# Experts' token transposes moved behind the up products, two experts ahead

## What is computed

```python
xn = layernorm(x)
attn = einsum('bsr,or->bso', rfs(xn, xis, exp(xis), proj), rfs(iw, xis, exp(xis), proj))
# mixture of experts
scores = sigmoid(tokens @ router_w)            # 4 of 8 groups, then 8 of 64 experts
dispatch = dispatch.at[flat_e, pos_c].add(tokens[tidx] * valid[:, None])   # 256 rows an expert
g = einsum('ech,ehi->eci', dispatch, gate_w)   # 512 -> 256
u = einsum('ech,ehi->eci', dispatch, up_w)     # 512 -> 256
expert_out = einsum('eci,eih->ech', silu(g) * u, down_w)                   # 256 -> 512
output = zeros.at[tidx].add(gathered * weights)
output = output + (silu(tokens @ sg) * (tokens @ su)) @ sd
return x + attn + output
```

## Time and profile before

| | |
|---|---|
| median of 3 runs | 1327.19 us (1311.12 to 1372.49) |
| profiled execution | 1307.97 us |
| its span | 1306.2 us |
| granted TensorE clock, mean | 0.996 |
| PE busy | 1280.0 us (98%) |
| DVE busy | 916.0 us (70%) |
| ACT busy | 647.3 us (50%) |
| POOL busy | 433.9 us (33%) |
| moved by DMA | 263.65 MB, mean 202 GB/s |
| DMA rate in the experts' half | 277 to 298 GB/s by slice |

### The profile page before, as it was taken

The page is one execution under the profiler, slowest core; times in us unless marked ns, Lnnn a source line. Parts: engine busy times, 40 slices in busy tenths (PEclk is TensorE's granted clock), DMA queues, the critical chain, the costliest instruction groups (busy, mean ns, idle before and its releaser), DMA issues.

```text
span 1306.2 us, 22561 instructions
## 1 busy us (share of the span) xinstructions
PE 1280.0 (98%) x7565; PEld 1123.8 (86%) x7565; DVE 916.0 (70%) x1787; ACT 647.3 (50%) x1053; POOL 433.9 (33%) x344
## 2 busy tenths in 40 slices
PE   6999999999999999999999999999999999999995
PEld 5888888888888888888889999999999999999994
DVE  7878877777777777785656667667766766676662
ACT  4421232212322123221256777777877777777772
POOL 1000000000000000000014666777666667676653
PEclk9999999999999999999999999999999999999998
DMA  7336554664546645445447999999999999999995
GB/s 269 121 107 163 130 121 127 157 166 98 130 119 153 167 104 131 114 118 134 134 133 214 286 278 286 287 290 292 290 291 285 298 291 287 282 295 285 298 277 65
DMA packets 203800, 263.65 MB, mean 202 GB/s; under 512 B 49268, under 2 KB 138744, under 8 KB 203768
## 3 DMA queue, kind: packets, MB, share of 16 engines
q1 hardware_dynamic: 175096, 191.93, 50.9%
q0 software_dynamic: 28672, 71.32, 23.7%
HBM read 178.18 MB, written 71.39 MB: 191 GB/s over the span
## 4 chain that ended last, share of the span: by engine, by line
PE 96%; DVE 2%; DMA 1%; ACT 0%; issue 0%; POOL 0%; SPq 0%; ACTq 0%
PE pmm L1255 18%; PE pmm L1257 18%; PE pmm L1256 18%; PE pout L1255 11%; PE pout L1257 11%; PE pout L1256 11%; PE ptr L1488 4%; PE plog L1316 2%; PE plog L1325 1%; PE ptr L1267 0%; DMA out_dram<-outs,slot_cols 0%; DVE stats L829 0%; DMA xbuf<-_L_attn_proj_matrix_dram 0%; DVE xt_lo L795 0%; PE plog L1345 0%
## 5 line engine op out<-in xcount | busy, mean ns | idle before, releaser
L1614 POOL DMA_INDIRECT out_dram<-outs,slot_cols x128 | 228.7, 1787 | 165.6 <-DMA out_dram<-outs,slot_cols 136.2
L1255 PE MATMUL pmm<-xt_hi,proj_hi 128*128 128x256 f32 (+1 forms) x784 | 253.0, 323 | 2.2 <-DVE xt_lo L795 1.4
L1257 PE MATMUL pmm<-xt_hi,proj_lo 128*128 128x256 f32 (+1 forms) x784 | 249.6, 318 | 0.0
L1256 PE MATMUL pmm<-xt_lo,proj_hi 128*128 128x256 f32 (+1 forms) x784 | 249.6, 318 | 0.0
L1255 PE MATMUL pmm<-xt_hi,sgu_hi 128*128 128x256 f32 (+1 forms) x768 | 246.1, 320 | 0.2 <-issue 0.2
L1256 PE MATMUL pmm<-xt_lo,sgu_hi 128*128 128x256 f32 (+1 forms) x768 | 243.4, 317 | 0.0
L1257 PE MATMUL pmm<-xt_hi,sgu_lo 128*128 128x256 f32 (+1 forms) x768 | 243.4, 317 | 0.0
L1598 POOL TENSOR_TENSOR earlier<-earlier,chosen 128x64 bf16<-128x64 bf16 x64 | 23.9, 373 | 617.8 <-DVE chosen L916 614.0
L1604 POOL DMA_INDIRECT xbuf<-rows,slot_cols x128 | 175.3, 1369 | 80.8 <-issue 38.6
L552 ACT ACTIVATE feat<-pmm,ab 128x512 f32<-128x512 f32 x68 | 46.7, 687 | 292.4 <-PE pmm L1257 286.4
L1255 PEld LDWEIGHTS pmm<-xt_hi,proj_hi 128*128 128x128 f32 x784 | 147.3, 188 | 13.6 <-ACT feat L552 1.6
(11 more groups left out here) (185 smaller groups left out, 2543.7 us busy)
## 6 DMA issues: line engine op xcount, KB each, us to landing
raw<-in_L_ffn_gate_w_dram SPq DMA_DIRECT2D x64, 512.0 KB
raw<-in_L_ffn_up_w_dram SPq DMA_DIRECT2D x64, 512.0 KB
raw<-in_L_ffn_down_w_dram SPq DMA_DIRECT2D x64, 512.0 KB
outs<-in_L_attn_x_dram SPq DMA_DIRECT2D x32, 512.0 KB, 3.9
out_dram<-outs SPq DMA_DIRECT2D x32, 512.0 KB, 3.0
xbuf<-in_L_attn_x_dram SPq DMA_DIRECT2D x52, 256.0 KB, 7.6
raw<-xn SPq DMA_DIRECT2D x52, 256.0 KB, 6.2
rows<-raw SPq DMA_DIRECT2D x39, 256.0 KB, 4.2
```

What stands on the lines that cost most here:

```text
L1255: pe.matmul(psum, lh, rh, start=first and n == 0, stop=False)
L1256: pe.matmul(psum, lh, rl, start=False, stop=False)
L1257: ins = pe.matmul(psum, ll, rh, start=False, stop=final and n == len(pairs) - 1)
L1614: pool.indirect_dma_start(out=out, out_offset=bass.IndirectOffsetOnAxis(ap=slot_cols[:, at:at + 1], axis=0), in_=outs[e.b][:, c, :], in_of ...
```

## The change

The transposes move in the queues of three engines, and are made one expert further ahead. On TensorE they stand between the up products and the down products, for expert e + 2. On ScalarE the copy to `xt_hi` stands behind the rounding of the down weights; on VectorE `xt_lo` stands behind the hidden product, and the down weights' residual moves ahead of the hidden product. The first two sets of transposes are read out ahead of the first stage, and the last stages leave theirs out.

```diff
--- before.py
+++ after.py
@@ -738,12 +738,12 @@
                         e_out_made, 1)
 
             def stage(e, next_rows=True, next_weights=True, out_prev=True, look=None):
-                if next_rows:
-                    e_turned_hi(e.next())
                 if next_weights:
                     gate_up_hi(e.next())
                 e_silu(e)
                 down_hi(e)
+                if next_rows:
+                    e_turned_hi(e.next().next())
                 e_hidden_hi(e)
                 if out_prev:
                     e_out(e.prev())
@@ -751,6 +751,7 @@
                     sum_signs(look)
 
             e_turned_hi(turn(0))
+            e_turned_hi(turn(1))
             stage(turn(0), next_weights=False, out_prev=False)
             for b in range(2):
                 act.wait_ge(out_stored[b], 16 * GROUPS)
@@ -759,7 +760,7 @@
                 for k in range(CHUNK):
                     stage(four(2 * m + 1, k), look=m + 2 if k == 1 else None)
             for n in range(E - 6, E - 1):
-                stage(turn(n))
+                stage(turn(n), next_rows=n < E - 2)
             stage(turn(E - 1), next_rows=False, next_weights=False)
             e_out(turn(E - 1))
 
@@ -1224,18 +1225,19 @@
                                   ALU.subtract).then_inc(e_hid_lo_made, 1)
 
             def stage(e, next_rows=True, next_weights=True, look=None):
-                if next_rows:
-                    e_turned_lo(e.next())
                 if next_weights:
                     gate_up_lo(e.next())
+                down_lo(e)
                 e_hidden(e)
-                down_lo(e)
+                if next_rows:
+                    e_turned_lo(e.next().next())
                 e_hidden_lo(e)
                 if look is not None:
                     look[0](look[1])
 
             e_turned_lo(turn(0))
             output(turn(GROUPS - 1), 3)
+            e_turned_lo(turn(1))
             stage(turn(0), next_weights=False)
             stage(turn(1))
             with dve.Fori(0, CHUNKS - 2) as m:
@@ -1520,18 +1522,20 @@
             pe.wait_ge(out_free, 2 + J * GROUPS)
             e_turn(turn(2))
             e_gate_up(turn(1))
+            e_turn(turn(3))
             e_down(turn(0))
             with pe.Fori(0, CHUNKS - 2) as m:
                 for k in range(CHUNK):
                     e = four(2 * m + 1, k)
-                    e_turn(e.next())
                     e_gate_up(e)
                     if k == 1:
                         look_up(m + 2)
+                    e_turn(e.next().next())
                     e_down(e.prev())
             for n in range(E - 6, E - 1):
-                e_turn(turn(n + 1))
                 e_gate_up(turn(n))
+                if n < E - 2:
+                    e_turn(turn(n + 2))
                 e_down(turn(n - 1))
             e_gate_up(turn(E - 1))
             e_down(turn(E - 2))
```

## The result

The kernel got slower. Before: median 1310.72 us (1308.82 to 1372.49, 6 executions). After: 1354.55 us (1337.07 to 1404.95, 6 executions). The ratio, formed from the undisturbed executions alone, is 1.0245, 95% interval 1.0152 to 1.0338. The profiled execution took 1337.07 us, its span 1335.4 us, against 1306.2: 29.2 us more. The executions of the changed kernel lie far apart (68 us). The kernel before has outliers too, but a common level: of 57 later ones, 47 lie between 1307.51 and 1313.53, the others between 1324 and 1361. The changed kernel was run ten times in all and has no such level; its times spread over 1335 to 1405.

A forecast was written before the change was run, and what follows sets the result against it. TensorE, a queue that hardly stops, bounds the kernel, with GpSimd's chain of adds close behind. 0 + 2.1 + 0 + 2.7 + 4 = 8.8 us gave 1317 on the profiled run, 1336 on the median; stated 1331, range 1309 to 1357.

The forecast's parts named there:

- rival 1: Adds' lag grows back each stage, TensorE waits 0.47 us at each set of transposes: 30 us, 1338 profiled; chance 0.18.
- the place on TensorE: Transposes between up and down products cost what they did before: 0, bounds 5 us gain and 0.6 us loss.
- the wait at the start: First stage: residual delays expert 0's hidden product, so expert 1's gate products start at 700.29 against 698.22: +2.1 us, once.
- the clock: TensorE's clock: transposes don't count as busy, their number stays the same, so it changes no term.
- the hidden product after a look-up: VectorE, stage after a look-up: hidden product done 923.60, before gate products at 923.85; cost 0, cover 0.15 us.
- rival 3: Hidden product late after look-ups if ScalarE's or VectorE's operations stretch 0.3 us more: 4.5 us on top, 1322; chance 0.10.
- loads 2 us earlier: Residual ahead of the hidden product frees the down weights' buffer sooner, so weight loads are issued about 2 us earlier.
- +2.7, a wait of TensorE needs to be paid once: Transposes miss gathered rows by at most 2.7 us; one wait uses up the adds' lag, then rows are in time.
- +4, a sixth of 25: Adds' lag could grow 0.47 us a stage over 54 stages; earlier weight loads counter it, so +4 us taken.
- large near the tenth to fourteenth expert and small or absent later: Expected sign in the profile after: TensorE's waits for a gather at the transposes, by expert.
- time from gather issue to use: From the end of the second gather issue to the transposes: 8.15 and 7.48 us before, 4.5 and 3.9 after.
- the 25: Full cost if the adds' lag grows back over 54 later stages, 0.47 us each: 25 us.

The follow-up runs named there:

- half loads: Changed kernel, from expert 3 on only half the columns of the gate, up and down weights loaded: 1310.55 us, ratio 0.9995.
- half adds: Changed kernel with each expert's second add left out, so half the experts' results are missing: 1306.96 us, ratio 0.998.
- gather first: Changed kernel, GpSimd issues the gather of expert n ahead of the adds of n - 5, not behind them: 1322.78 us, ratio 1.0098.
- four buffers: Changed kernel, four row buffers for two, gathers ahead of adds: 1324.10 us, ratio 1.0106; with the first hidden product ahead of the residual again: 1318.69 us, 1.007.
- both runs with half of the change: Kernel before with only VectorE's residual moved ahead of the hidden product: ratio 1.0038; changed kernel with only that move undone: ratio 1.0163.
- the swap alone: Kernel before, VectorE computes the down weights' residual ahead of the hidden product, transposes unmoved: 1314.07 us, ratio 1.0038.
- one expert ahead: Changed kernel with the next expert's transposes at the new place, instead of those two experts on: 1330.99 us, ratio 1.0154.
- the second profile of the changed kernel: Changed kernel run again unedited, four executions, 1334.85 to 1396.54 us; the profiled one 1368.92 us, no ratio formed.
- Without the swap: Changed kernel with VectorE's hidden product ahead of the down weights' residual again, transposes as changed: 1329.13 us, ratio 1.0163.
- the loads held: Changed kernel, SyncE holds loads until the hidden product's residual of two experts before is computed, some 3.5 us later: 1337.63 us, ratio 1.0213.

## Why the prediction was right and wrong

The range held and the direction too, but with luck: 1331 was stated, 1337.07 was the profiled time and 1354.55 the median. The range, 1309 to 1357, was this wide only because rival 1, at a chance of 0.18, gave its upper end, and 1331 lies near the profiled time because it was set between two levels. The ratio of 1.00 to 1.01 was missed (1.0245), and the sum did not hold: 8.8 us were predicted on the span, 29.2 measured.

**Right: the place on TensorE, 0.** With no wait left, four stages take 37.59 us (half loads, half adds) against 37.64: a gain of 0.8 us over the half (1.4 by the time between the fourth and the last transposes, 562.4 us against 563.8), between the bounds given.

**Right: the wait at the start, +2.1; missing: what follows it.** The changed kernel, VectorE and TensorE:

```profile
698.05 1.23 DVE L1198 TENSOR_TENSOR sdn_lo<-raw,sdn_hi 128x1024 fp32r<-128x1024 f32 x1 [1.56 <-ACT sdn_hi L716]
699.20 0.68 DVE L1219 TENSOR_TENSOR hid<-gate_t,pmm 128x512 f32<-128x512 f32 x1
```
```profile
699.98 0.36 PE L1257 MATMUL pmm<-xt_hi,sgu_hi 128*128 128x256 f32 x1 [2.27 <-issue]
```

Hidden product done at 699.88 (700.22 predicted), gate products behind it, 2.27 us of idleness; it answers to the earlier trace rows. Behind it the granted clock fell to 0.50 for some of the next products, and the 48 gate and up products took 7.16 us (699.98 to 707.14) instead of 5.66 (710.79 to 716.45): 1.5 us more. The prediction had no term for the clock.

**Right: the hidden product after a look-up, 0 with little cover.** 0.25 us of cover and 0.1 of handing over were worked out. In the changed kernel:

```profile
891.53 0.68 DVE L1219 TENSOR_TENSOR hid<-gate_t,pmm 128x512 f32<-128x512 f32 x1
```
```profile
892.46 0.28 PE L1257 MATMUL pmm<-xt_hi,sgu_hi 128*128 128x256 f32 x1
```

892.46 - 892.21 = 0.25, no wait. The warning was sound: where the result copies came late (gather first, four buffers), this cover failed, and that is rival 3.

**Right: loads 2 us earlier.** The down load is issued 5.9 to 6.4 us behind the first gate product in three of four stages, 8.5 in the fourth, 7.9 before.

**Wrong: "+2.7, a wait of TensorE needs to be paid once".** The step that failed is its reason, that the chain of adds does not wait for TensorE. It was true of the kernel before. Here the adds catch up, as both runs with half of the change show (lag 1.3 and 1.1 us), until they start 0.2 us behind the result copies, and result copies follow TensorE. From then on, by the order of the queues, a wait at the transposes delays down products, copies, adds and the next gather by as much: it buys no slack. Waits came 22 times, 20.9 us, the largest 2.1; and each puts some 0.2 us on top, since the first transposes' weights load behind it (last product's start to the transposes 0.28 instead of 0.12 beside the wait, transposes to the next product 0.84 instead of 0.79).

**Wrong: "+4, a sixth of 25".** It weighed a lag that grows from stage to stage against earlier loads, and took both as smooth. The lag did not grow in quiet stretches (0.4 us on average over the first 16 experts) and jumped to 5 us in a long one. In place of 2.7 + 4 = 6.7 us stand 25.9 us more between the fourth and the last transposes (589.7 us against 563.8), of which 16.5 go with the chain of adds. The parts add up: 562.4 us for these sixty stages where nothing waits (half loads), 20.9 of waits, 22 x 0.21 = 4.6 on top, and 1.6 for one stretch at half clock make 589.5. Rival 1 had the size, 30 us and 1338 on the profiled run, with the wrong pace: not 0.47 us in each stage, but two regimes. Its beat of 9.8 us is there only as the mean of all sixty stages (9.83); quiet stretches run at 9.55, the long one at 10.37.

**Wrong by the expected rows:** waits "large near the tenth to fourteenth expert and small or absent later". The first is 0.52 us at the ninth, the largest 2.1 at the forty-first. The time from gather issue to use was also taken too short (3.9 to 4.5 us; at 869.75 it is 7.2, of which 0.75 are the wait), because adds that start sooner take their gathers with them, and so were landings (4.7 to 6.6 us; median 6.7).

The rule of the Trainium skill quoted from "DMA: Bandwidth & Descriptors", section "Issuing engines are not separate DMA queues", was said to speak for the 25, not the 4. The runs agree that transfers of different issuers share something: with half of the loads, transfers of SyncE's queue, adds issued by GpSimd land 1.4 us sooner. But with the swap alone, which starts the loads earlier, the adds' lag fell from 2.5 to 1.3 us and the stages took 564.3 us against 563.8: that is the way the 4 assumed, and the 25 didn't come from there.

**Not in the sum: the clock.** The prediction let it change no term. The kernel before has no stretch at the lower level between the start of the experts and TensorE's last product, the changed one has two, 1.5 and 1.6 us dear, each behind a wait of over 2 us.

## What to carry to other kernels

An engine at 98% with a chain right behind it has a second bound. Before a consumer is moved nearer to its data, ask what sets the pace of the producer: if the producer follows the consumer, through copies, adds and a buffer, a wait is not paid once but each time the landing varies. A chain that waits for landings on full DMA engines has no fixed time; leave it the slack of its slowest landing, and look at several executions, because one profile can show only one of two regimes. And slack can be moved, not made: a gather put ahead of the adds took away all waits for rows, and part of the time was lost again at result copies and look-ups, and at the very end, where the late adds land after all products are done. When a loss is split into parts, add the parts up against the span: what is missing points at a cost that no wait shows, here the clock and the end.

## What the runs showed of the hardware

A wait can cost the clock as well. After the wait of 2.27 us at the start the granted clock was 0.50 from 702 to 704, which is the 1.2 GHz level; after the wait of 2.10 us ahead of the transposes at 1072.64 it was 0.50 from 1074 to 1076, and 1.00 from 1078 on (stretches in us: PE, PEld, DVE, ACT and POOL busy, granted clock, DMA share, GB/s):

```profile
702.00:704.00 2.00, 2.00 (x11) 2.00 (x11) 2.00 (x2) 0.68 (x1) 1.68 (x1) 0.50 1.01 344
...
1074.00:1076.00 2.00, 2.00 (x7) 1.61 (x6) 0.37 (x2) 1.54 (x2) 1.50 (x2) 0.50 1.00 240
1076.00:1078.00 2.00, 2.00 (x10) 1.61 (x9) 2.00 (x4) 0.69 (x1) 1.05 (x1) 0.90 0.92 227
1078.00:1080.00 2.00, 2.00 (x19) 2.00 (x18) 1.12 (x2) 1.87 (x3) 0.00 (x0) 1.00 1.14 248
```

The eight transposes took 1.68 us instead of 1.09, and with the down products behind them 1.6 us more than elsewhere. After the wait of 1.90 us at 1050.20 nothing of the kind is seen, and of the other 20 waits at the transposes none shows it. Nor does each wait as long as these: the start's wait of 2.1 to 2.3 us stands in ten profiles, and the clock fell behind it in seven (not with the swap alone, not one expert ahead, not in the second profile of the changed kernel). Without the swap it fell at the waits of 2.01 and 2.36 us; with the loads held, waits of 3.45 and 3.19 us were followed by 1.00. What decides was not found.

In the long stretch transfers start close together and land late, though less is moved: the DMA share is 0.93 (1020 to 1058) against 1.03 in the kernel before, the rate 243 GB/s against 297, and yet an expert's adds take 10 to 11 us from first issue to landed, where 7.5 to 10 is usual. So full engines alone don't explain the long landings of this stretch. That the bunching is the cause was not shown: the run with loads held back didn't tell.
